# Reordering the steps of a software pipeline for multi-group cross-attention on one core

## The chip, the cores and the metric

The kernel runs on one core of a Trainium2 chip. The metric is the device time of one execution in microseconds (us). The engines are named as the profile names them: PE is the matrix engine (PEld its weight loads), ACT the scalar engine, DVE the vector engine, POOL the GpSimd engine, and SP issues DMAs. Each engine runs its own instruction list in order; they wait for one another through semaphores.

## What is computed

`x` is (16, 512, 640) and the context is (16, 512, 1024). Twenty heads of 32 channels attend to four groups of context tokens, each with its own key and value weights and its own softmax:

```python
q = _heads(hidden_states @ to_q_w)
h_txt = _sdpa(q, _heads(ehs_txt @ to_k_w), _heads(ehs_txt @ to_v_w))               # 77 tokens
h_obj = _sdpa(q, _heads(ehs_obj @ to_k_object_w), _heads(ehs_obj @ to_v_object_w)) # 4
h_oth = _sdpa(q, _heads(ehs_oth @ to_k_others_w), _heads(ehs_oth @ to_v_others_w)) # 4
h_ip = _sdpa(q, _heads(ehs_ip @ to_k_ip_w), _heads(ehs_ip @ to_v_ip_w))            # 427
out = _merge(h_txt) + _merge(h_obj) + _merge(h_oth) + _merge(h_ip)
out = out @ to_out_w + to_out_b + hidden_states
```

All of it is float32. Products with weights, and the scores, are made precise by splitting each operand into a high and a low part and adding three partial products.

## The kernel before, in words

There are two programs one behind the other. `project_context` makes all keys and values and takes the first 934 us of the span; the change does not touch it. `attend` does the rest. It works on 80 units; a unit is one batch with one block of 128 channels, which is four heads.

A unit passes through these operations:

- `queries`: 15 matmuls of 512 columns into the one PSUM tile `m_ps` (L845). `keep_queries` on DVE (L1032, L1035) scales them and splits them into `q_out`; its second instruction raises the semaphore `q_lo`. SP then copies them into `qpack` (L681).
- `scores`: 8 pairs of matmuls into the double buffer `s_ps` (L796), with the query tokens on the partitions. For each pair `pair_max` on DVE takes the row maximum (L984) and copies the 85 columns of the three small groups to `small` (L991); `ip_sums` on ACT takes the exponentials of the 427 columns of the last group and sums them (two L926 activations, each with a read of the accumulator).
- the small groups, in two halves: `small_max` on DVE (L998, L999), `less_max` on POOL (L766, L767), `small_exp` on ACT (L934), `small_sums` on DVE (L1005, L1006).
- `logs_of` on ACT (L943), `neg_lse` and `turn_lse` on DVE (L1012 to L1025), and `pack_lse` on SP, which puts the negated logarithm of the sums into extra rows of `qpack` (L688).
- `scores_t`: the scores again, now transposed and less the logarithm, 8 pairs of matmuls ("duos") into the single buffer `st_ps` (L810); `prob` on ACT takes their exponentials (L918).
- `values`: 4 times 4 matmuls with probabilities against values into `o_ps` (L824, two passes each in the trace); `heads_hi` and `heads_lo` on DVE split the result (L1045, L1050).
- `output`: 15 matmuls of 512 columns into the same `m_ps` (L868), nine slots after the unit's queries; `add_output` on DVE (L1057) adds bias and residual and raises `y_added`.

The order is written out by hand. Each engine runs `slot(m)` for m from 0 to 88, and each slot has eight steps, k from 0 to 7. A slot holds the work of one unit at each stage of the pipeline: queries of unit m, scores of units m-2 and m-1, transposed scores of m-4 and m-3, values of m-4, output of m-9. On PE a step is one duo of `scores_t`, at even steps one block of `values`, then one pair of `scores`, with pieces of `queries` and `output` at the places that the tables `Q_AHEAD`, `Q_BEHIND`, `Y_AHEAD` and `Y_BEHIND` name (ahead of that pair, or behind it). Each table maps a step to a range of the 15 products. On ACT a step is `prob` and `ip_sums`; on DVE it is `pair_max`.

Since queries and outputs share `m_ps`, they alternate. The first product of an output waits until DVE has taken the queries out (`q_lo`), and the first product of the next queries waits until DVE has taken the output out (`y_added`). A pair of `scores` waits for the exponentials of the pair two before it (`s_exp`), and a duo of `scores_t` waits for the exponentials of the duo before it (`p_done`).

## Time and profile before

| | |
|---|---|
| median of 3 runs | 2585.89 us (2582.41 to 2586.15) |
| the profiled execution | 2585.89 us, span 2584.0 us |
| busy over the span | PE 97%, PEld 71%, ACT 66%, DVE 62%, POOL 16% |
| busy from 1162 us on, by 40 slices of the span | PE, ACT and DVE at 9 tenths nearly throughout |

The span is the time from the first to the last instruction; the remaining 1.9 us lie around it. The figures over the span mix the two programs: ACT and DVE are little used in the first and heavily in the second. A row of the timeline is: start in us, duration in us, engine, line, operation, what it writes and reads, the number of instructions merged into the row and, in brackets, how long the engine had been idle and what released it. Consecutive instructions of an engine overlap in the records (a matmul's record includes its way through the array), so the pace of an engine is the distance between starts, not the sum of durations.

### The profile page before, as it was taken

To read this page: it belongs to the slowest core of one execution; us is meant where nothing else is said; L and a number is where in the kernel's file an instruction comes from. 1 tells how busy PE (TensorE), PEld (TensorE's weight loads), DVE (VectorE), ACT (ScalarE), POOL (GpSimd) and SP (SyncE) were. 2 spreads that over 40 slices of the span, in tenths; PEclk is the share of its full clock that TensorE was granted. 3 is DMA by queue.
4 is the path that set the end of the run, shared out by engine and by line. 5 is a ranking of instruction groups with operands and counts; after the bars stand their busy time and mean duration, and the time that the engine had idled before them with its cause. 6 is when DMAs were issued, how large, how long until landed. Compare 5 with 4: busy or idle time off the path is not lost.

```text
span 2584.0 us, 37371 instructions
## 1 busy us (share of the span) xinstructions
PE 2495.0 (97%) x13125; PEld 1844.4 (71%) x13125; DVE 1605.4 (62%) x2964; ACT 1707.9 (66%) x3830; POOL 408.5 (16%) x564
## 2 busy tenths in 40 slices
PE   8999999999999956999999999999999999999997
PEld 7999999999999944456666666666666666666654
DVE  3131111112121127889999999999999999999991
ACT  3131212212121116999999999999999999999992
POOL 0000000000000021321321321321321231232210
PEclk9999999999999987899999999999999999999999
DMA  9473333233232235666666666766776676666741
GB/s 235 127 243 125 119 115 122 102 119 114 95 130 96 102 106 114 120 131 126 147 147 126 149 149 123 157 143 124 153 146 124 149 147 134 143 142 139 141 101 59
DMA packets 287618, 341.25 MB, mean 132 GB/s; under 512 B 89406, under 2 KB 181694, under 8 KB 287430
## 3 DMA queue, kind: packets, MB, share of 16 engines
q1 hardware_dynamic: 234032, 275.93, 47.8%
q10 hardware_dynamic: 53398, 62.93, 7.4%
q8 instruction: 104, 1.70, 0.3%
q14 instruction: 84, 0.69, 0.1%
HBM read 186.71 MB, written 83.89 MB: 105 GB/s over the span
## 4 chain that ended last, share of the span: by engine, by line
PE 57%; ACT 3%; DVE 1%; DMA 1%; issue 1%; SPq 0%; DVEq 0%
PE s_ps L796 13%; PE st_ps L810 12%; PE o_ps L824 12%; PE m_ps L845 11%; PE m_ps L868 10%; ACT s_ps L926 2%; ACT probs L918 1%; DVE kpack L970 0%; DVE negmax L984 0%; DMA qpack<-q_out 0%; DMA small<-in_group_rows 0%; ACT small L934 0%; DMA out<-in_xT 0%; DVE out L1057 0%; DVE wo L975 0%
## 5 line engine op out<-in xcount | busy, mean ns | idle before, releaser
L926 ACT ACTIVATE s_ps<-s_ps,negmax 128x427 f32<-128x427 f32 x1280 | 762.0, 601 | 43.9 <-DVE small L991 43.9
L984 DVE TENSOR_REDUCE negmax<-s_ps 128x2 f32<-128x854 f32 x640 | 667.0, 1042 | 85.2 <-PE s_ps L796 85.0
L918 ACT ACTIVATE probs<-st_ps 128x1024 f32<-128x1024 f32 x640 | 662.4, 1035 | 57.7 <-PE st_ps L810 51.6
L796 PE MATMUL s_ps<-kpack,qpack 96*128 96x512 f32 x1280 | 438.9, 425 | 25.5 <-ACT s_ps L926 19.4
L464 PE MATMUL v_ps<-w_split,ctx_split 128*128 128x320 f32 (+2 forms) x3072 | 453.7, 309 | 1.5 <-DVE w_split L386 1.5
L464 PEld LDWEIGHTS v_ps<-w_split,ctx_split 128*128 128x128 f32 (+2 forms) x3072 | 451.4, 186 | 2.5 <-DVE w_split L386 1.8
L447 PE MATMUL k_ps<-ctx_split,w_split 128*128 128x428 f32 (+2 forms) x2280 | 428.0, 349 | 5.1 <-DVE ctx_split L386 4.6
L810 PE MATMUL st_ps<-qpack,kpack 104*128 104x512 f32 x1280 | 418.1, 408 | 13.6 <-ACT probs L918 12.7
L447 PEld LDWEIGHTS k_ps<-ctx_split,w_split 128*128 128x128 f32 x2280 | 409.6, 189 | 21.0 <-DVE ctx_split L386 4.9
L796 PEld LDWEIGHTS s_ps<-kpack,qpack 96*128 96x128 f32 x1280 | 215.8, 192 | 281.8 <-ACT s_ps L926 236.9
L391 DVE TENSOR_TENSOR k_out<-k_ps,k_out 128x427 fp32r<-128x427 f32 (+2 forms) x97 | 56.0, 578 | 532.9 <-ACT k_out L287 532.9
L766 POOL TENSOR_TENSOR small<-small,negmax 128x616 f32<-128x616 f32 x160 | 196.1, 1226 | 1162.5 <-DVE negmax L999 1162.5
L845 PE MATMUL m_ps<-xs,wq 128*128 128x512 f32 x1200 | 349.9, 401 | 26.3 <-DVE wq L975 24.8
L824 PE MATMUL o_ps<-probs,vt 128*32 128x512 f32 x2560 | 346.0, 613 | 1.1 <-ACT probs L918 1.1
L810 PEld LDWEIGHTS st_ps<-qpack,kpack 104*128 104x128 f32 x1280 | 228.8, 191 | 151.1 <-ACT probs L918 103.2
L868 PE MATMUL m_ps<-heads,wo 128*128 128x512 f32 x1200 | 317.4, 396 | 5.3 <-DVE out L1057 3.7
L308 ACT ACTIVATE v_out<-v_ps 128x640 f32<-128x640 f32 (+1 forms) x64 | 45.2, 706 | 386.6 <-PE v_ps L464 386.6
L845 PEld LDWEIGHTS m_ps<-xs,wq 128*128 128x128 f32 x1200 | 231.4, 193 | 82.2 <-issue 25.0
L926 ACT ACTIVATION_READ_ACCUMULATOR s_ps<-s_ps,negmax 128x1 f32 x1280 | 281.0, 220 | 0.0
L868 PEld LDWEIGHTS m_ps<-heads,wo 128*128 128x128 f32 x1200 | 224.7, 190 | 63.3 <-issue 5.7
L287 ACT ACTIVATE k_out<-k_ps 128x427 fp32r<-128x427 f32 (+2 forms) x97 | 49.2, 507 | 280.0 <-PE k_ps L447 262.3
L991 DVE COPY small<-s_ps 128x170 f32<-128x170 f32 x640 | 207.3, 324 | 0.0
(54 smaller groups left out, 1437.7 us busy)
## 6 DMA issues: line engine op xcount, KB each, us to landing
kpack<-kT SPq DMA_DIRECT2D x240, 256.0 KB, 5.0
qpack<-q_out SPq DMA_DIRECT2D x240, 256.0 KB, 5.7
kT<-k_out ACTq DMA_DIRECT2D x160, 217.5 KB, 2.2
ctx_split_raw<-in_ctxT SPq DMA_DIRECT2D x128, 214.0 KB, 4.5
xs_raw<-in_xT SPq DMA_DIRECT2D x80, 256.0 KB, 4.9
out<-in_xT SPq DMA_DIRECT2D x80, 256.0 KB, 5.7
out_yT<-out SPq DMA_DIRECT2D x80, 256.0 KB, 3.4
v_ip_rows<-v_out ACTq DMA_DIRECT2D x48, 320.0 KB
```

The costliest lines, as they stand in the source:

```text
L447: last = nc.tensor.matmul(k_place(run, m)[:, 0:n], w[W[name][0]][:, pw, q, m * P:(m + 1) * P], c[run % 2][:, px, q, a:a + n], start=(q == ...
L464: last = nc.tensor.matmul(v_ps[0:rows, v0 % 2, half, 0:CH // 2], c[run % 2][:, px, q, a:a + rows], w[W[name][0]][:, pw, q, half * (CH // 2 ...
L766: nc.gpsimd.tensor_tensor(txt, txt, over_keys(m_txt, N_TXT), ALU.add).then_inc(sm_sub, 1)
L796: last = nc.tensor.matmul(s_ps[:, n % 2, z, :], qpack[0:ROWS_S, r, j, t * P:(t + 1) * P], kpack[0:ROWS_S, r, j, :], start=True, stop=True)
L810: last = nc.tensor.matmul(st_ps[:, z, :], kpack[0:ROWS_ST, r, j, kt * P:(kt + 1) * P], qpack[0:ROWS_ST, r, j, :], start=True, stop=True)
L824: last = nc.tensor.matmul(o_ps[j * HD:(j + 1) * HD, :], vt[:, r, kt, j * HD:(j + 1) * HD], probs[:, (ITEMS * u + HPU * kt + j) % PR, :], s ...
L845: last = nc.tensor.matmul(m_ps[:, :], wq[:, pw, c, cols], xs[:, px, c, :], start=(n == 0), stop=(n == PRODUCTS - 1))
L868: last = nc.tensor.matmul(m_ps[:, :], wo[:, pw, z, cols], heads[:, (w // QC * QC + z) % HR, po, :], start=(n == 0), stop=(n == PRODUCTS - 1))
L918: nc.scalar.activation(probs[:, at:at + 2, :], st_ps[:, :, :], ACT.Exp).then_inc(p_done, 1)
L926: last = nc.scalar.activation(s_ps[:, n % 2, z, SMALL:TOK], s_ps[:, n % 2, z, SMALL:TOK], ACT.Exp, bias=negmax[:, r, IP, j, t:t + 1], accu ...
L984: nc.vector.tensor_reduce(negmax[:, r, IP, j, t0:t0 + 2], s_ps[:, n % 2, :, SMALL:TOK], AX_X, ALU.max, negate=True).then_inc(s_max, 1)
L991: nc.vector.tensor_copy(small[:, w:w + 2, :], s_ps[:, n % 2, :, 0:SMALL]).then_inc(s_max, 1)
```

## The change

Nothing is computed differently. The order of the steps of a slot changes on all five engines:

- PE: pieces of `queries` and `output` are all placed ahead of the pair of scores, in runs of 7, 2 and 6 (queries, steps 5, 6, 7) and 6, 2 and 7 (output, steps 1, 2, 3). The fourth block of `values` (step 6) goes ahead of the pair as well.
- DVE: `heads_hi` moves from the start of step 0 of the next slot to the start of step 7, and `heads_lo` behind step 7's `pair_max`; `small_max` and `small_sums` of the first half and `add_output` each move one step later, `small_max` of the second half too.
- ACT: `small_exp` runs behind steps 4 and 7 and not behind steps 3 and 0; `logs_of` at step 2 and not 1.
- POOL: `less_max` at steps 4 and 7, behind `split_x`; the last chunk of `x` is split at step 5.
- SP: three chunks of the next batch of `x` are loaded behind `pack_keys`, and the last two at the start of the next slot, ahead of `pack_queries`.

```diff
-Q_AHEAD = {5: (4, 8), 7: (11, 13)}
-Q_BEHIND = {4: (0, 4), 5: (8, 11), 7: (13, 15)}
-X_STEPS = {0: (0,), 1: (1,), 2: (2,), 3: (3,), 4: (4,)}
+Q_STEPS = {5: (0, 7), 6: (7, 9), 7: (9, 15)}
+X_STEPS = {0: (0,), 1: (1,), 2: (2,), 3: (3,), 5: (4,)}
-Y_AHEAD = {1: (0, 5), 3: (10, 15)}
-Y_BEHIND = {1: (5, 10)}
+Y_STEPS = {1: (0, 6), 2: (6, 8), 3: (8, 15)}
@@ sync, slot
+                if m > 0 and m % QC == 0 and unit(m):
+                    load_x(m, range(X_EARLY, QC))
                 if unit(m - 1):
                     pack_queries(m - 1)
...
-                if (m + 1) % QC == 0 and unit(m + 1):
-                    load_x(m + 1, range(X_EARLY))
                 if m > 0 and unit(m):
                     pack_keys(m)
                 if (m + 1) % QC == 0 and unit(m + 1):
-                    load_x(m + 1, range(X_EARLY, QC))
+                    load_x(m + 1, range(X_EARLY))
@@ gpsimd, slot
-                    if k in (3, 6) and unit(m - 2):
-                        less_max(m - 2, k // 6)
                     if m % QC == 0 and unit(m):
                         for c in X_STEPS.get(k, ()):
                             split_x(m, c)
+                    if k in (4, 7) and unit(m - 2):
+                        less_max(m - 2, k // 7)
@@ tensor
+            def products_at(m, k):
+                if k in Q_STEPS and unit(m):
+                    queries(m, range(*Q_STEPS[k]))
+                if k in Y_STEPS and unit(m - Y_LAG):
+                    output(m - Y_LAG, range(*Y_STEPS[k]))
...
-                    if k in (0, 2, 4) and unit(m - 4):
+                    if k % 2 == 0 and unit(m - 4):
                         values(m - 4, k // 2)
-                    products_at(m, k, Q_AHEAD, Y_AHEAD)
+                    products_at(m, k)
                     u, p = pair_at(m, k + 1) if k + 1 < STEPS else pair_at(m + 1, 0)
                     if unit(u):
                         scores(u, p)
-                    products_at(m, k, Q_BEHIND, Y_BEHIND)
-                    if k == 6 and unit(m - 4):
-                        values(m - 4, k // 2)
@@ scalar, slot
-                    if k == 1 and unit(m - 3):
+                    if k == 2 and unit(m - 3):
                         logs_of(m - 3)
...
-                    if k == 0 and unit(m - 3):
-                        small_exp(m - 3, 1)
-                    if k == 3 and unit(m - 2):
-                        small_exp(m - 2, 0)
+                    if k in (4, 7) and unit(m - 2):
+                        small_exp(m - 2, k // 7)
@@ vector, slot
-                    if k == 0 and unit(m - 5):
-                        heads_hi(m - 5)
-                        heads_lo(m - 5)
+                    if k == 7 and unit(m - 4):
+                        heads_hi(m - 4)
...
-                    if k in (2, 5) and unit(m - 2):
-                        small_max(m - 2, k // 5)
-                    if k == 3 and unit(m - Y_LAG):
+                    if k in (3, 6) and unit(m - 2):
+                        small_max(m - 2, k // 6)
+                    if k == 4 and unit(m - Y_LAG):
                         add_output(m - Y_LAG)
-                    if k == 4 and unit(m - 2):
+                    if k == 5 and unit(m - 2):
                         small_sums(m - 2, 0)
+                    if k == 7 and unit(m - 4):
+                        heads_lo(m - 4)
```

The first place is PE around the boundary of two slots, from the pair of scores that step 7 issues (it is the pair of the next slot's step 0) to the first product of the output. Before:

```order
L796 MATMUL s_ps<-kpack,qpack 128x512 [waits s_exp]
L796 MATMUL s_ps<-kpack,qpack 128x512
L845 MATMUL m_ps<-xs,wq 128x512 x2
L810 MATMUL st_ps<-qpack,kpack 128x512 [waits p_done]
L810 MATMUL st_ps<-qpack,kpack 128x512
L824 MATMUL o_ps<-probs,vt 32x512 [waits p_done,o_lo,v_in2]
L824 MATMUL o_ps<-probs,vt 32x512 x3
L796 MATMUL s_ps<-kpack,qpack 128x512 [waits s_exp]
L796 MATMUL s_ps<-kpack,qpack 128x512
L810 MATMUL st_ps<-qpack,kpack 128x512 [waits p_done]
L810 MATMUL st_ps<-qpack,kpack 128x512
L868 MATMUL m_ps<-heads,wo 128x512 [waits q_lo,o_lo]
```

And after:

```order
L843 MATMUL m_ps<-xs,wq 128x512 x6
L794 MATMUL s_ps<-kpack,qpack 128x512 [waits s_exp]
L794 MATMUL s_ps<-kpack,qpack 128x512
L808 MATMUL st_ps<-qpack,kpack 128x512 [waits p_done]
L808 MATMUL st_ps<-qpack,kpack 128x512
L822 MATMUL o_ps<-probs,vt 32x512 [waits p_done,o_lo,v_in1]
L822 MATMUL o_ps<-probs,vt 32x512 x3
L794 MATMUL s_ps<-kpack,qpack 128x512 [waits s_exp]
L794 MATMUL s_ps<-kpack,qpack 128x512
L808 MATMUL st_ps<-qpack,kpack 128x512 [waits p_done]
L808 MATMUL st_ps<-qpack,kpack 128x512
L866 MATMUL m_ps<-heads,wo 128x512 [waits q_lo,o_lo]
```

The last two products of the queries stood between the pair of scores and the output; now all of them stand ahead of the pair.

The second place is DVE over the same boundary, from the pair of step 7 to the queries. L984 and L991 (after: L977 and L984) are one `pair_max`. Before:

```order
L984 TENSOR_REDUCE negmax<-s_ps 128x2 [waits s_done]
L991 COPY small<-s_ps 128x170
L1045 CAST heads<-o_ps 128x512 [waits y_done,pv_done]
L1050 TENSOR_TENSOR heads<-o_ps,heads 128x512 [waits o_hi]
L984 TENSOR_REDUCE negmax<-s_ps 128x2 [waits s_done]
L991 COPY small<-s_ps 128x170
L1032 TENSOR_SCALAR q_out<-m_ps 128x512 [waits q_packed1,q_acc]
L1035 SCALAR_TENSOR_TENSOR q_out<-m_ps,q_out 128x512 [waits q_hi]
```

And after:

```order
L1038 CAST heads<-o_ps 128x512 [waits y_done,pv_done]
L977 TENSOR_REDUCE negmax<-s_ps 128x2 [waits s_done]
L984 COPY small<-s_ps 128x170
L1043 TENSOR_TENSOR heads<-o_ps,heads 128x512 [waits o_hi]
L977 TENSOR_REDUCE negmax<-s_ps 128x2 [waits s_done]
L984 COPY small<-s_ps 128x170
L1025 TENSOR_SCALAR q_out<-m_ps 128x512 [waits q_packed1,q_acc]
L1028 SCALAR_TENSOR_TENSOR q_out<-m_ps,q_out 128x512 [waits q_hi]
```

The two parts of the heads have moved apart, around step 7's pair; step 0's pair is still the last thing ahead of the queries.

The third place is ACT from the second half's exponential (L929 after) to the logarithm. Before, the exponential stands one step ahead of the logarithm and behind step 0's pair; after, it stands behind step 7's pair:

```order
L929 ACTIVATE small<-small 128x680 [waits sm_sub]
L913 ACTIVATE probs<-st_ps 128x1024 [waits pv_done,st_done]
L921 ACTIVATE s_ps,sums<-s_ps,negmax 128x427 [waits s_max]
L921 ACTIVATE s_ps,sums<-s_ps,negmax 128x427
L913 ACTIVATE probs<-st_ps 128x1024 [waits pv_done,st_done]
L921 ACTIVATE s_ps,sums<-s_ps,negmax 128x427 [waits s_max]
L921 ACTIVATE s_ps,sums<-s_ps,negmax 128x427
L913 ACTIVATE probs<-st_ps 128x1024 [waits pv_done,st_done]
L938 ACTIVATE logs<-sums 128x64 [waits lse_step,s_exp,sm_sum]
```

The exponential now stands directly ahead of step 0's `prob`, and two more `prob` lie between it and the logarithm.

## Rows read from the trace of the kernel before

**Rows 1.** Windows: engines' busy us, then granted clock, DMA share and GB/s.
```profile
1143.00:1162.00 19.00, 19.00 (x98) 11.75 (x94) 17.47 (x34) 18.49 (x44) 8.54 (x11) 1.00 0.80 177
```

**Rows 2.** Timeline, DVE, the first half of keep_queries in four slots.
```profile
1019.84 0.68 DVE L1032 TENSOR_SCALAR q_out<-m_ps 128x512 fp32r<-128x512 f32 x1
...
1123.63 0.68 DVE L1032 TENSOR_SCALAR q_out<-m_ps 128x512 fp32r<-128x512 f32 x1
...
1162.00 0.68 DVE L1032 TENSOR_SCALAR q_out<-m_ps 128x512 fp32r<-128x512 f32 x1
...
2486.83 0.68 DVE L1032 TENSOR_SCALAR q_out<-m_ps 128x512 fp32r<-128x512 f32 x1
```

**Rows 3.** Timeline, PE, from step 7 to step 1 of the next slot.
```profile
1525.03 0.62 PE L796 MATMUL s_ps<-kpack,qpack 96*128 96x512 f32 x2
...
1525.96 0.63 PE L810 MATMUL st_ps<-qpack,kpack 104*128 104x512 f32 x2
1526.53 1.07 PE L824 MATMUL o_ps<-probs,vt 128*32 128x512 f32 x8
1527.52 0.73 PE L796 MATMUL s_ps<-kpack,qpack 96*128 96x512 f32 x2
1528.10 0.63 PE L810 MATMUL st_ps<-qpack,kpack 104*128 104x512 f32 x2
1528.56 1.33 PE L868 MATMUL m_ps<-heads,wo 128*128 128x512 f32 x5
1529.73 0.40 PE L796 MATMUL s_ps<-kpack,qpack 96*128 96x512 f32 x1
```

**Rows 4.** Timeline, PEld, the weight loads of the first output products.
```profile
1528.42 1.04 PEld L868 LDWEIGHTS m_ps<-heads,wo 128*128 128x128 f32 x5
```

**Rows 5.** Timeline, DVE, from heads_lo to the queries of that boundary.
```profile
1525.02 0.69 DVE L1050 TENSOR_TENSOR heads<-o_ps,heads 128x512 fp32r<-128x512 f32 x1
1525.69 1.05 DVE L984 TENSOR_REDUCE negmax<-s_ps 128x2 f32<-128x854 f32 x1
1526.65 0.33 DVE L991 COPY small<-s_ps 128x170 f32<-128x170 f32 x1
1526.89 0.68 DVE L1032 TENSOR_SCALAR q_out<-m_ps 128x512 fp32r<-128x512 f32 x1
1527.61 0.69 DVE L1035 SCALAR_TENSOR_TENSOR q_out<-m_ps,q_out 128x512 fp32r<-128x512 f32 x1
```

**Rows 6.** Timeline, the first unit: products that waited for keep_queries.
```profile
961.94 0.69 DVE L1035 SCALAR_TENSOR_TENSOR q_out<-m_ps,q_out 128x512 fp32r<-128x512 f32 x1
962.68 1.46 PEld L845 LDWEIGHTS m_ps<-xs,wq 128*128 128x128 f32 x7 [2.01 <-DVE q_out L1035]
```

**Rows 7.** Timeline, PE and ACT, a prob that waited for its duo.
```profile
1521.96 0.63 PE L810 MATMUL st_ps<-qpack,kpack 104*128 104x512 f32 x2
1522.63 1.02 ACT L918 ACTIVATE probs<-st_ps 128x1024 f32<-128x1024 f32 x1 [0.35 <-PE st_ps L810]
```

**Rows 8.** Timeline, ACT, steps 0 and 1 of a slot.
```profile
1507.66 1.03 ACT L918 ACTIVATE probs<-st_ps 128x1024 f32<-128x1024 f32 x1
1508.57 0.61 ACT L926 ACTIVATE s_ps<-s_ps,negmax 128x427 f32<-128x427 f32 x1
...
1509.75 0.80 ACT L934 ACTIVATE small<-small 128x680 f32<-128x680 f32 x1
1510.41 1.05 ACT L918 ACTIVATE probs<-st_ps 128x1024 f32<-128x1024 f32 x1
```

**Rows 9.** Timeline, SP's issue of pack_lse.
```profile
1513.77 2.96 SPq L688 DMA_DIRECT2D qpack<-lse_t  x4
```

**Rows 10.** DMA share in 40 slices of 1507 to 1527 us, in tenths.
```profile
DMA  0000001999998999983210200399678997898999
```

**Rows 11.** Windows of two slots without output, columns as in rows 1.
```profile
1060.00:1079.00 19.00, 17.04 (x83) 8.56 (x79) 17.05 (x33) 18.58 (x44) 2.99 (x4) 1.00 0.58 101
1079.00:1101.00 22.00, 20.46 (x79) 10.35 (x79) 16.81 (x32) 18.35 (x43) 2.99 (x4) 0.77 0.47 86
```

More of the change, by code:

```diff
@@ L871, in output @@
                     last.then_inc(y_done, 1)
-            def products_at(m, k, q_at, y_at):
-                if k in q_at and unit(m):
-                    queries(m, range(*q_at[k]))
-                if k in y_at and unit(m - Y_LAG):
-                    output(m - Y_LAG, range(*y_at[k]))
+            def products_at(m, k):
[3 more added lines that the diff above has]
+                    output(m - Y_LAG, range(*Y_STEPS[k]))
             def slot(m):
```

## The prediction, made before the changed kernel ran

> **What bounds the kernel now.** I read the windows first. In 1143 to 1162 us, a stretch of the part in which every stage of the pipeline has a unit, PE is busy 19.00 of 19.00 us at a granted clock of 1.00, ACT 18.49 and DVE 17.47 [rows 1]. That is too close to call from busy shares, so the second view is the cadence: the first half of `keep_queries` runs once per slot, at 1162.00 and, 69 slots later, at 2486.83 [rows 2], so a full slot takes 1324.83 / 69 = 19.20 us. The third is the timeline of PE, to see whether those 19.20 us are work or waits. Two matmuls of 512 columns take 0.46 to 0.47 us from start to start (1528.10 to 1528.56, and 1525.03 to 1525.96 for four), five take 1.17 (1528.56 to 1529.73), 0.234 each. A duo ahead of values takes 0.57, a block of values 0.99, and the pair behind it 0.58, 0.11 more than a pair elsewhere, because its first weight load has nothing to hide behind [rows 3]. A slot has 16 matmuls of scores, 16 of transposed scores and 30 products, so 62 x 0.234 = 14.5 us, and 4 blocks of values at (0.57 - 0.47) + 0.99 + 0.11 = 1.2, 4.8 us: 19.3, the cadence. So in a full slot PE never waits; 19.20 us is its floor. Slots without output are another matter: there PE is busy 17.04 of 19.00 us, and the clock is at 1.00 in one and at 0.77 in the next [rows 11].
>
> **What the change can't win.** It removes no instruction from PE, and puts the same number of blocks of values between 128-row matmuls, so each full slot keeps the 19.20 us floor. The evener spread over the steps is of use to ACT and DVE alone, and neither is the bound. So the sum has only costs in it, but for the slots at the start and the end.
>
> **The cost: the hand-over of `m_ps`.** The first product of the output waits for `q_lo`, which `keep_queries` raises behind step 0's `pair_max`. I measure both sides from the pair of scores that this `pair_max` reads (S0, 1525.03).
> - DVE: `pair_max` starts 0.66 behind S0 (1525.69), the queries 1.20 behind that (1526.89), their second instruction 0.72 later (1527.61) and lasts 0.69 [rows 5]. The end is at S0 + 3.27.
> - PE before: two products, duo, values, pair, duo, then the output's first product at 1528.56, S0 + 3.53 [rows 3]. Its weight load starts at 1528.42, 0.12 behind the end of the DVE instruction [rows 4, 5]. It fits with next to nothing to spare.
> - PE after: no products behind S0. The path is pair 0.47, duo 0.57, values 0.99, pair 0.58, duo 0.46: S0 + 3.07. That is 0.20 ahead of the end of `keep_queries`; DVE's side is unchanged, since `pair_max` still stands ahead of the queries and starts when S0 is done.
>
> So PE now waits in every slot that has both a `keep_queries` and an output. Release to weight load was 0.05 where products did wait for this instruction (962.63 to 962.68) [rows 6] and 0.12 in rows 4 and 5; the exposed first load costs 0.11, taken from the pair behind values [rows 3]. The stall is 3.27 + 0.05 + 0.11 - 3.07 = 0.36 to 3.27 + 0.12 + 0.11 - 3.07 = 0.43; I take the middle, 0.395. The bounds are wider: with the handover at 0.05 and no refill it is 0.25, and if the whole 0.26 from the DVE end to the product's own start (1528.30 to 1528.56) is needed and the refill comes on top, 0.57. The slots are m = 9 (the first output) to 80 (the last `keep_queries`), 72 of them: 72 x 0.395 = 28.4 us, bounds 18 to 41. Nothing gives it back: all that stands behind the waiting product on PE (scores for DVE, duos for ACT) comes later by as much.
>
> **Edits that I cost at nothing, and their cover.** Slot times below count from step 0's duo, with the stall.
> - `small_exp` ahead of step 0's `prob`, and `heads_hi` (0.7) ahead of step 7's `pair_max`. From step 7's pair (S7): `pair_max` + 0.66, some 0.1 late for `heads_hi`, 1.3 to the end of its copy [rows 5], ACT's two activations 1.18, `small_exp` 0.66 [rows 8], `prob` 1.03 and about 0.15 to the next duo: 5.1 us to step 1's duo. PE's own way from S7 to it is 0.47 + 0.47 + 6 x 0.234 + 0.47 + 0.57 + 0.99 + 0.58 = 4.95. It is about 0.15 late, and right behind it is the product that waits 0.395 anyway: hidden. Were that stall not there, it would cost 0.15, 11 us in all.
> - `small_exp` behind step 4. Duo 4 to its `prob` 0.67 [rows 7], `prob` 0.91, activations 1.18, `small_exp` 0.66 [rows 8], `prob` to duo 6 1.18: 4.60. PE's way: 0.57 + 0.99 + 0.58 + 0.46 + 7 x 0.234 + 0.47 = 4.71. Margin 0.11, the thinnest.
> - Elsewhere a duo allows the next after 0.67 + 1.18 = 1.85, and the shortest step is 2.1.
> - `add_output` one step later. From the pair of step 4 to the first product of the next queries PE's way is again 3.07; DVE's is the chain above with one instruction where `keep_queries` has two: 3.27 - 0.72 + 0.23 = 2.78. Margin 0.29.
> - The fourth block of values ahead of its pair moves 1.2 us of work by one place. It waits for step 5's `prob`, which ends some 0.7 ahead of it by the walk above.
> - The logarithm one step later: `pack_lse` is issued at 1513.77 before, 7.0 us into its slot, over 2.96 us [rows 9], and the duo that needs it is at 1521.96 [rows 7], 15.2 into it. After, `prob` of step 2 starts at about 4.9 + 0.67 and ends 1.05 later, so the issue starts at about 8.1 and ends at 11.1; the duo comes at 14.7. Before, the DMA engines are idle from 1517.5 us, within 1.3 of the end of the issue at 1516.73 [rows 9, 10]; so the rows land by 12.4, with 2.3 us to spare.
> - `load_x` past `pack_keys`, its last two chunks ahead of `pack_queries` every fifth slot: `pack_queries` waits for `q_lo` until 2.8 us into the slot, and issuing two loads and the residual takes less. The chunks are multiplied at step 5 or later, over 12 us into the slot. POOL is busy 8.54 of 19 us in such a stretch [rows 1]: its moved steps are hidden.
>
> The Trainium skill ("DMA: Bandwidth & Descriptors", Queues, rings and completion order) says that on each DMA engine descriptors are consumed in ring order. By it the logarithms' packets, in every fifth slot, stand behind two more chunks of `x`. Rows 10 agree in kind: the share stays at 8 or 9 tenths until the queries are through and only then falls. By the rule the landing moves later in 16 slots; it changes no term of the sum.
>
> **Slots without output, and the tail.** The five slots from 1019.84 to 1123.63 take 103.8 us [rows 2], some near 19 us and some near 22 at the lower clock [rows 11]. ACT's 18.58 [rows 11] is their new floor at best, up to half a microsecond a slot under 19. If all keep the full clock, 5 x 19 = 95 is 9 less; if all lose it, 5 x 22 = 110 is 6 more. I take -1, with both ends in the range. After slot 80 no queries are left, so the wait on `q_lo` is gone; tail 0, give or take 2.
>
> **The sum.** Profiled execution 2585.9 (span 2584.0, the rest around it; the median of the runs is the same 2585.89) + 28.4 - 1 = 2613.3; predicted 2613 us.
>
> **The rivals.**
> - A second stall besides: the margin of 0.11 at step 6 is made of sums of rows to 0.01 and of ACT's pace, which is not constant. If it fails by 0.1 to 0.3 a slot, 7 to 22 us come on top, as they are at another place of PE's order: 2620 to 2635. For it: three engines within 1 us of each other. Against it: the margin holds with the rows as they are.
> - The clock. The stall makes PE idle once a slot, and rows 11 show a slot at 0.77 taking 22 us and not 19. If this came in full slots, 72 x 3 = 216 on top: about 2830. Against it: in 1060 to 1079 PE was idle 2 us of 19 and the clock stayed at 1.00; after the change it idles 0.4 of 19.6. The Trainium skill ("TensorE: Matmul & The Clock Gate", A second HAM failure mode: psum-queue depth-cycling) says that frequent micro-idles between groups of matmuls can make the clock oscillate; by it this rival would be the likely one. The rows bear it out for slots with five times the idle time, and not in each of those.
> - The logarithms late. All that is certain of their landing is that it was no later than the duo at 1521.96, 5.2 us behind the issue. If it took all of that, the duo would wait until 16.3 instead of 14.7: 1.6 x 80 = 128 us, about 2742. Rows 10 speak against it.
> - The wait is hidden: if PE ran a little behind its pace between S0 and the output, or the queries were taken out earlier, the change would only shuffle work under PE's floor: 2583 to 2588.
> - Faster: the evener steps free the slots without output. There PE idles, and the 11 products of steps 4 and 5 make ACT wait; spread over three steps they would not. With the full clock all through it is 9 us and with ACT's floor 2 more: 2575. It wins only if the stall at `m_ps` stays under 11 / 72 = 0.15 us a slot, below both my bounds.
>
> **Chances.** The forecast 0.62 (its own range 2602 to 2624), second stall 0.20, clock 0.03, logarithms 0.04, hidden 0.06, faster 0.05. What a measurement of this kernel can tell from no change is about 0.2%, 5 us. So slower 0.62 + 0.20 + 0.03 + 0.04 = 0.89, same 0.06, faster 0.05. The range runs from the forecast's end, less some for the start's clock, to the end of the second stall: 2598 to 2638, which leaves out about 0.18.
>
> **What would show it.** The distance between two `keep_queries` in full slots should be 19.6 and not 19.20. In the waits, PE's output line should appear as waiting for DVE's second `q_out` instruction in about 72 slots, 0.2 to 0.6 us each, as before it did not. The granted clock should stay 1.00 from 1162 us on. Waits of duos for `prob` should not grow beyond step 1's. If the cadence is 19.20, the reading of the hand-over is wrong; if it is above 19.7, there is a second stall, and the duo of step 6 is the first place to look.

## The result and the profile after

The changed kernel takes 2628.45 us (median of 4 runs, 2625.99 to 2630.26), the kernel before 2586.02 in the same session (4 runs, 2582.41 to 2596.81): a ratio of 1.0156, 95% interval 1.0126 to 1.0187. It is slower by 42.4 us. Forecast were 27 more, 2613: the direction held, and so did the whole range, 2598 to 2638. The range of the forecast proper, 2602 to 2624, did not: 15 us of the cost were not in the sum.

The profiled execution of after took 2634.56 us (span 2632.5), 6 more than the median; the accounts below are of this one execution against the one before, and so add up to a little more than 42.4.

Busy times over the span, to be held against the small table of before: the work is the same, only the span has grown from 2584.0 to 2632.5 us.

```profile
PE 2526.2 (96%) x13125; PEld 1843.3 (70%) x13125; DVE 1621.9 (62%) x2964; ACT 1716.9 (65%) x3830; POOL 408.0 (15%) x564
```

A window over one full slot, columns as in [rows 1]:

```profile
1199.80:1219.40 19.60, 19.56 (x98) 11.76 (x94) 17.57 (x35) 18.82 (x44) 3.00 (x4) 1.00 0.64 126
```

The granted clock is 1.00, so the time is not lost to the clock. PE counts as 19.56 busy of 19.60 although it waits in this slot, as shown below: a matmul's record covers its way through the array, and short waits vanish in it. The starts tell more. `keep_queries` [rows 2], now L1025, in the timeline of DVE: slot 10, four around one batch boundary, and slot 80.

```profile
1139.54 0.68 DVE L1025 TENSOR_SCALAR q_out<-m_ps 128x512 fp32r<-128x512 f32 x1
...
1417.61 0.68 DVE L1025 TENSOR_SCALAR q_out<-m_ps 128x512 fp32r<-128x512 f32 x1
...
1437.21 0.68 DVE L1025 TENSOR_SCALAR q_out<-m_ps 128x512 fp32r<-128x512 f32 x1
...
1458.88 0.68 DVE L1025 TENSOR_SCALAR q_out<-m_ps 128x512 fp32r<-128x512 f32 x1
...
1478.49 0.68 DVE L1025 TENSOR_SCALAR q_out<-m_ps 128x512 fp32r<-128x512 f32 x1
...
2530.98 0.68 DVE L1025 TENSOR_SCALAR q_out<-m_ps 128x512 fp32r<-128x512 f32 x1
```

The distances are 19.60, 21.67 and 19.61. Four full slots of five take 19.60, as forecast; the first slot of each batch takes 20.6 to 21.7. From slot 10 to slot 80 it is 1391.44 us, which is 70 x 19.60 + 19.4, so each of the 14 batch starts costs 1.39 on top. Before, slot 10's stood at 1142.80:

```profile
1142.80 0.68 DVE L1032 TENSOR_SCALAR q_out<-m_ps 128x512 fp32r<-128x512 f32 x1
```

and slot 80's at 2486.83 [rows 2]: 1344.03. The accounts: loop +47.4 (28.0 of it 70 x 0.40, and 19.4 for the batch starts), slot 10 reached 3.3 earlier, the tail behind slot 80's `keep_queries` 4.4 longer (101.5 against 97.1): 48.5, the difference of the spans.

**The ordinary slot.** PE over the boundary, to be held against [rows 3]:

```profile
1515.82 0.63 PE L794 MATMUL s_ps<-kpack,qpack 96*128 96x512 f32 x2
1516.28 0.63 PE L808 MATMUL st_ps<-qpack,kpack 104*128 104x512 f32 x2
1516.85 1.06 PE L822 MATMUL o_ps<-probs,vt 128*32 128x512 f32 x8
1517.84 0.73 PE L794 MATMUL s_ps<-kpack,qpack 96*128 96x512 f32 x2
1518.47 0.73 PE L808 MATMUL st_ps<-qpack,kpack 104*128 104x512 f32 x2
1519.24 1.62 PE L866 MATMUL m_ps<-heads,wo 128*128 128x512 f32 x6
1520.71 0.62 PE L794 MATMUL s_ps<-kpack,qpack 96*128 96x512 f32 x2
```

The end of the queries on DVE [rows 5], and the weight load released by it [rows 4]:

```profile
1517.69 0.68 DVE L1025 TENSOR_SCALAR q_out<-m_ps 128x512 fp32r<-128x512 f32 x1
1518.41 0.69 DVE L1028 SCALAR_TENSOR_TENSOR q_out<-m_ps,q_out 128x512 fp32r<-128x512 f32 x1
```
```profile
1519.21 1.23 PEld L866 LDWEIGHTS m_ps<-heads,wo 128*128 128x128 f32 x6 [0.45 <-issue]
```

From S0 at 1515.82, DVE is through at S0 + 3.28 and the load starts 0.11 later. The duo ahead of the product starts at 1518.47 and the product at 1519.24, 0.77 later, where [rows 3] have 0.46: 0.31 of the 0.40. The duo of step 1 starts 0.63 behind its pair and not 0.58, because `prob` is a little late: 0.05. Its weight load waited for that:

```profile
1518.46 0.30 PEld L808 LDWEIGHTS st_ps<-qpack,kpack 104*128 104x128 f32 x2 [0.33 <-ACT probs L913]
```

The rest is refill: the six products take 1.47 from start to start and not 6 x 0.234 = 1.40. The three add up to 0.43; the remainder of the slot runs 0.03 quicker than before, which leaves the 0.40. The profile puts the 0.45 down to "issue", not to `q_out`, so the waits view doesn't name the semaphore; the order of starts does.

**The batch start.** DVE at step 2 of such a slot, on which nothing was to change:

```profile
1440.89 1.05 DVE L977 TENSOR_REDUCE negmax<-s_ps 128x2 f32<-128x854 f32 x1 [0.25 <-PE s_ps L794]
...
1442.56 1.27 DVE L1005 TENSOR_TENSOR neglse<-negmax,logs 128x64 f32<-128x64 f32 x1 [0.38 <-ACT logs L938]
1443.86 0.52 DVE L1008 CAST neglse<-neglse 128x64 fp32r<-128x64 f32 x1
1444.42 1.40 DVE L1010 TENSOR_TENSOR neglse<-neglse 128x64 fp32r<-128x64 f32 x1
1445.85 0.31 DVE L1018 STREAM_TRANSPOSE lse_t<-neglse 128x128 f32<-128x128 f32 x1
1446.08 1.01 DVE L977 TENSOR_REDUCE negmax<-s_ps 128x2 f32<-128x854 f32 x1
```

The three small instructions of `neg_lse` take 3.3 us from 1442.56 to 1445.82. The same ones before, in a batch start:

```profile
1531.82 0.21 DVE L1012 TENSOR_TENSOR neglse<-negmax,logs 128x64 f32<-128x64 f32 x1
1532.07 0.22 DVE L1015 CAST neglse<-neglse 128x64 fp32r<-128x64 f32 x1
1532.33 0.28 DVE L1017 TENSOR_TENSOR neglse<-neglse 128x64 fp32r<-128x64 f32 x1
```

0.8 us. And POOL, in the batch start after:

```profile
1440.54 1.28 POOL L755 TENSOR_TENSOR xs<-xs_raw,xs 128x512 fp32r<-128x512 f32 x1
1441.78 0.60 POOL L753 CAST xs<-xs_raw 128x512 fp32r<-128x512 f32 x1
1442.46 1.29 POOL L755 TENSOR_TENSOR xs<-xs_raw,xs 128x512 fp32r<-128x512 f32 x1
1443.69 0.61 POOL L753 CAST xs<-xs_raw 128x512 fp32r<-128x512 f32 x1
1444.38 1.29 POOL L755 TENSOR_TENSOR xs<-xs_raw,xs 128x512 fp32r<-128x512 f32 x1
```

POOL's subtractions end at 1443.75 and 1445.67, DVE's two at 1443.83 and 1445.82: each of DVE's ends about 0.1 after POOL's, whatever its own work. Before, POOL was idle then: it waited in `less_max` for `row_max`, which DVE makes behind `neg_lse`, and the splits stood behind that.

```profile
1528.33 1.30 POOL L757 TENSOR_TENSOR xs<-xs_raw,xs 128x512 fp32r<-128x512 f32 x1
1533.83 1.23 POOL L766 TENSOR_TENSOR small<-small,negmax 128x616 f32<-128x616 f32 x1 [4.21 <-DVE negmax L999]
...
1535.28 0.61 POOL L755 CAST xs<-xs_raw 128x512 fp32r<-128x512 f32 x1
```

From there the delay goes on by data. ACT waits 2.40 for `pair_max`, and PE for ACT:

```profile
1447.37 0.59 ACT L921 ACTIVATE s_ps<-s_ps,negmax 128x427 f32<-128x427 f32 x1 [2.40 <-DVE small L984]
```
```profile
1448.72 0.73 PE L794 MATMUL s_ps<-kpack,qpack 96*128 96x512 f32 x2 [1.28 <-ACT s_ps L921]
```

Two theories to be tested, then. H: the hand-over of `m_ps` costs 0.4 in every full slot. P: at batch starts POOL's `split_x` holds up DVE's `neg_lse`, since the edits (split 3 ahead of `less_max`, chunks loaded later) brought them together. A third edit, the logarithm a step later, moves `neg_lse` only a little: it starts 5.34 us behind `keep_queries` after and 4.92 before, and this edit was not tested by itself. The texts of what was expected, written before each run, call H theory A and P theory C. Their rival B puts the 0.40 down to the moved `small_exp` and `heads_hi`, and their rival D puts the long batch starts down to the order of SP's loads alone.

### The profile page after: what moved, and what is told of

It reads as the page before. It is cut to its first block, busy times and chain, and to the rows that moved or that the text cites. A ratio compares the mean times of both kernels' runs of the same rounds, so it can differ in the third digit from the quotient of the medians.

```text
span 2632.5 us, 37371 instructions
## 1 busy us (share of the span) xinstructions
PE 2526.2 (96%) x13125; PEld 1843.3 (70%) x13125; DVE 1621.9 (62%) x2964; ACT 1716.9 (65%) x3830; POOL 408.0 (15%) x564
## 4 chain that ended last, share of the span: by engine, by line
PE 54%; ACT 4%; DVE 4%; issue 2%; DMA 1%; SPq 0%; DVEq 0%
PE st_ps L808 11%; PE m_ps L843 11%; PE s_ps L794 11%; PE m_ps L866 11%; PE o_ps L822 10%; ACT probs L913 2%; ACT s_ps L921 2%; DVE negmax L977 1%; DVE neglse L1010 1%; DVE neglse L1005 0%; DVE neglse L1008 0%; DVE small L984 0%; DMA small<-in_group_rows 0%; DMA qpack<-q_out 0%; DVE kpack L963 0%
## 5 line engine op out<-in xcount | busy, mean ns | idle before, releaser
L977 DVE TENSOR_REDUCE negmax<-s_ps 128x2 f32<-128x854 f32 x640 | 665.3, 1039 | 126.7 <-PE s_ps L794 124.9
L794 PE MATMUL s_ps<-kpack,qpack 96*128 96x512 f32 x1280 | 426.2, 415 | 39.1 <-ACT s_ps L921 32.8
L794 PEld LDWEIGHTS s_ps<-kpack,qpack 96*128 96x128 f32 x1280 | 230.1, 191 | 227.1 <-issue 115.6
L843 PE MATMUL m_ps<-xs,wq 128*128 128x512 f32 x1200 | 331.6, 407 | 27.8 <-DVE wq L968 26.2
L866 PE MATMUL m_ps<-heads,wo 128*128 128x512 f32 x1200 | 332.1, 409 | 9.4 <-DVE out L1050 4.9
L843 PEld LDWEIGHTS m_ps<-xs,wq 128*128 128x128 f32 x1200 | 224.4, 193 | 140.1 <-issue 90.2
L866 PEld LDWEIGHTS m_ps<-heads,wo 128*128 128x128 f32 x1200 | 216.9, 191 | 143.7 <-issue 101.7
L984 DVE COPY small<-s_ps 128x170 f32<-128x170 f32 x640 | 207.5, 324 | 0.0
```

What stands on the lines that cost most here:

```text
L794: last = nc.tensor.matmul(s_ps[:, n % 2, z, :], qpack[0:ROWS_S, r, j, t * P:(t + 1) * P], kpack[0:ROWS_S, r, j, :], start=True, stop=True)
L843: last = nc.tensor.matmul(m_ps[:, :], wq[:, pw, c, cols], xs[:, px, c, :], start=(n == 0), stop=(n == PRODUCTS - 1))
L866: last = nc.tensor.matmul(m_ps[:, :], wo[:, pw, z, cols], heads[:, (w // QC * QC + z) % HR, po, :], start=(n == 0), stop=(n == PRODUCTS - 1))
L977: nc.vector.tensor_reduce(negmax[:, r, IP, j, t0:t0 + 2], s_ps[:, n % 2, :, SMALL:TOK], AX_X, ALU.max, negate=True).then_inc(s_max, 1)
L984: nc.vector.tensor_copy(small[:, w:w + 2, :], s_ps[:, n % 2, :, 0:SMALL]).then_inc(s_max, 1)
```

## The experiments

Each was timed on one chip with the kernel before, whose median was 2582.75 beside the first four experiments of the table, 2584.75 beside the next four and 2582.8 beside the last two. Kernels of different sessions are therefore compared by ratio or by the loop, which is the time from slot 10's `keep_queries` to slot 80's in the one profiled execution of each. All times are in us.

| | median (lowest to highest), runs | ratio to before, 95% | ordinary slot | loop |
|---|---|---|---|---|
| before | 2586.02 (2582.41 to 2596.81), 4 | | 19.20 | 1344.03 |
| after | 2628.45 (2625.99 to 2630.26), 4 | 1.0156 (1.0126 to 1.0187) | 19.60 | 1391.44 |
| a_two_behind | 2612.43 (2608.65 to 2616.77), 5 | 1.0108 (1.0091 to 1.0126) | 19.34 | 1377.04 |
| b_two_ahead | 2615.71 (2613.01 to 2618.62), 5 | 1.0122 (1.0105 to 1.0139) | 19.63 | 1373.92 |
| a_split_late | 2609.23 (2603.3 to 2613.61), 6 | 1.0095 (1.0076 to 1.0114) | 19.61 | 1376.32 |
| a_both | 2592.93 (2588.8 to 2597.4), 10 | 1.0035 (1.0023 to 1.0046) | 19.34 | 1358.08 |
| b_split_early | 2589.87 (2581.81 to 2592.82), 12 | 1.0015 (1.0002 to 1.0028) | 19.20 | 1349.25 |
| a_exp_back | 2596.25 (2594.83 to 2600.24), 6 | 1.0048 (1.0032 to 1.0064) | 19.34 | 1363.67 |
| a_loads_too | 2587.86 (2584.34 to 2591.09), 12 | 1.0008 (0.9997 to 1.002) | 19.34 | 1354.49 |
| a_queries_first | 2624.63 (2618.91 to 2626.03), 4 | 1.0151 (1.0131 to 1.0171) | 19.47 | 1388.66 |
| b_pool_meets | 2613.27 (2608.68 to 2615.28), 4 | 1.0107 (1.0083 to 1.0131) | 19.31 | 1371.24 |
| a_seven | 2578.35 (2575.46 to 2585.74), 12 | 0.998 (0.9968 to 0.9993) | 19.24 | 1347.19 |

**After, with two products of the queries back behind the pair (a_two_behind).**

```diff
-Q_STEPS = {5: (0, 7), 6: (7, 9), 7: (9, 15)}
+Q_STEPS = {5: (0, 7), 6: (7, 9), 7: (9, 13)}
+Q_BEHIND = {7: (13, 15)}
@@ tensor, slot, behind the pair of scores
+                    if k in Q_BEHIND and unit(m):
+                        queries(m, range(*Q_BEHIND[k]))
```

> The kernel after, with the last two query products of step 7 behind the pair of scores, as before. Theory A (the output's first product waits for keep_queries, because nothing stands behind the pair any more): PE's way from that pair to the product is 3.53 us again, the 0.40 us wait of each full slot shrinks to what the chain over small_exp to step 1's duo leaves, 0 to 0.15; cadence 19.20 to 19.35 instead of 19.60, the whole 18 to 29 us faster than the kernel after: 2600 to 2611. Rival B (the 0.40 comes from small_exp and heads_hi being moved to the boundary of two slots): cadence stays 19.60, time 2628. The extra 1.0 to 2.1 us of every fifth slot stays under both.

The ordinary slot fell from 19.60 to 19.34, the batch starts stayed long (about 1.7 each, 0.3 more than in after, which puts the time 1 us above the expected range). H holds for 0.26 of the 0.40; the rest is a second, smaller thing in the ordinary slot.

**Before, with the same two products ahead of the pair (b_two_ahead).** The one edit alone, in the kernel that has none of the others.

```diff
-Q_AHEAD = {5: (4, 8), 7: (11, 13)}
-Q_BEHIND = {4: (0, 4), 5: (8, 11), 7: (13, 15)}
+Q_AHEAD = {5: (4, 8), 7: (11, 15)}
+Q_BEHIND = {4: (0, 4), 5: (8, 11)}
```

> The kernel before, with one edit: the last two query products of step 7 ahead of the pair of scores. Theory A: the wait at the output's first product appears here alone, cadence 19.60 (19.55 to 19.65), no long fifth slots, 72 x 0.40 = 29 us slower than before: 2615. Rival B (it takes the moved exponential and heads): cadence 19.20, 2586.

19.63 in every slot, 0.43 over the floor, and no long batch starts: the loop is 29.9 longer. Nothing of `small_exp` or `heads_hi` has moved here, so rival B is out. Here the profile names the wait. Waits view, then the PE timeline with its pair S0 at 1513.93:

```profile
PE m_ps L868 <- DVE q_out L1035: 13.9, 68, 0.2
```
```profile
1513.93 0.63 PE L796 MATMUL s_ps<-kpack,qpack 96*128 96x512 f32 x2
...
1517.36 1.40 PE L868 MATMUL m_ps<-heads,wo 128*128 128x512 f32 x5 [0.20 <-DVE q_out L1035]
```

68 waits of up to 0.2 are booked, 13.9 us, under half of the 29.9 lost: the product starts at S0 + 3.43, where work alone would have it at 3.07 by the sum, 0.36 earlier.

**After, with chunks 3 and 4 both split at step 5, behind `less_max` (a_split_late).**

```diff
-X_STEPS = {0: (0,), 1: (1,), 2: (2,), 3: (3,), 5: (4,)}
+X_STEPS = {0: (0,), 1: (1,), 2: (2,), 5: (3, 4)}
```

> The kernel after, with chunk 3 of x split on POOL behind less_max of step 4 and not ahead of it (only X_STEPS changes). Theory C (in the first slot of a batch, split_x on POOL runs while DVE computes neg_lse on SBUF tiles, whose instructions then take up to 1.40 us instead of 0.28, and DVE passes it on to ACT and PE): the third instruction of neg_lse is back at 0.28 in all slots; the first stays long in some, since chunk 2 is still split there. The fifth slots' extra falls from 1.39 on the mean to 0 to 0.4, the time by 14 to 19 us: 2609 to 2615. Rival D (the extra comes from the order of SP's loads, chunks landing late): no change, 2628.

The loop is 15.1 shorter than after's (ratio 1.0095 for 1.0156), at an ordinary slot that stays at 19.61; the excess over 70 such slots falls from 19.4 to 3.6. One line's durations (least, median, most, in ns) say why; L1010 in after, then here:

```profile
L1010 DVE TENSOR_TENSOR neglse<-neglse x80: 270/278/1405, 1008.0 to 2575.7; 128x64 fp32r<-128x64 f32 x80
```
```profile
L1010 DVE TENSOR_TENSOR neglse<-neglse x80: 270/278/286, 1005.7 to 2555.9; 128x64 fp32r<-128x64 f32 x80
```

The medians are alike; only the largest shows that in after 14 of the 80 took 1.39 to 1.41 us. The loads come as late here as in after, so rival D, the loads alone, is out, and P holds. The first of the three instructions still met chunk 2's split in 12 slots.

**Both edits (a_both).** The two diffs above together.

> The kernel after with both edits (two products behind the pair, chunk 3 split late). Theories A and C together: 18 to 29 and 14 to 19 us off, 2583 to 2597, cadence 19.20 to 19.35. If one of the two rivals holds, 2600 to 2611 or 2609 to 2615; if both, 2628.

The single edits shortened the loop by 14.4 and 15.1, both together by 33.4. They add up and a little more: the batch starts, 1.39 long in after, were 1.7 in a_two_behind. H and P are two costs, nearly independent.

**Before, with chunk 3 split ahead of `less_max` (b_split_early).**

```diff
-X_STEPS = {0: (0,), 1: (1,), 2: (2,), 3: (3,), 4: (4,)}
+X_STEPS = {0: (0,), 1: (1,), 2: (2, 3), 4: (4,)}
```

> The kernel before, with chunk 3 of x split on POOL ahead of less_max of step 3 (only X_STEPS changes; SP's order of loads is that of before). Theory C: split_x of that chunk now runs when it lands, about 5 us into the first slot of a batch, where DVE computes neg_lse; its instructions lengthen from 0.21 to 0.28 to as much as 1.4 us in most of 15 slots, and these slots take 0.5 to 1.3 us longer: 7 to 19 us, 2590 to 2602. Rival D (it takes the new order of loads): no change, 2583.

Less than expected: the loop is 5.2 longer. With the early loads of before, chunk 2 is split soon enough, and only chunk 3 meets `neg_lse`. In 11 slots its split lengthens the first instruction, to 1.0 us at most; in three of these the subtraction then lengthens the second, the cast, from 0.22 to 1.33. The third is never touched.

```profile
L1012 DVE TENSOR_TENSOR neglse<-negmax,logs x80: 212/217/1004, 1001.6 to 2524.7; 128x64 f32<-128x64 f32 x80
```

The order on POOL alone is a part of the cause; the full cost needs the later loads too.

**After, with both edits and the second half's `small_exp` behind step 0 (a_exp_back).** Theory E: the 0.14 left in the ordinary slot is the late `prob` of step 0, because `small_exp` stands ahead of it.

```diff
-                    if k in (4, 7) and unit(m - 2):
-                        small_exp(m - 2, k // 7)
+                    if k == 0 and unit(m - 3):
+                        small_exp(m - 3, 1)
+                    if k == 4 and unit(m - 2):
+                        small_exp(m - 2, 0)
```

> a_both with small_exp of the second half back behind step 0 of the next slot. The cadence of 19.34 in a_both and a_two_behind is 0.14 over PE's 19.20. Theory E (that is the chain pair_max, exponentials, small_exp, prob to step 1's duo, worked out at 5.1 us against 4.95): without small_exp in it the chain is 0.66 shorter and the cadence 19.20; 72 x 0.14 = 10 us less than a_both: 2583. Rival F (the hand-over of m_ps still costs 0.14): cadence stays 19.34, 2593.

E fails: still 19.34. The wait went from the duo of step 1 to that of step 2, behind ACT's longer step 0. The rival F of the expectation, that the hand-over still costs this 0.14, is no better: the first product of the output starts 0.47 behind its duo, as it does without a wait. The PE timeline at step 2, with the weight load of the duo:

```profile
1507.94 0.62 PE L795 MATMUL s_ps<-kpack,qpack 96*128 96x512 f32 x2
1508.45 0.30 PEld L809 LDWEIGHTS st_ps<-qpack,kpack 104*128 104x128 f32 x2 [0.33 <-ACT probs L916]
1508.46 0.73 PE L809 MATMUL st_ps<-qpack,kpack 104*128 104x512 f32 x2
1509.12 1.06 PE L823 MATMUL o_ps<-probs,vt 128*32 128x512 f32 x8
```

The duo is 0.52 behind its pair and not 0.47, and the values 0.66 behind the duo and not 0.57: a wait of 0.05 costs 0.14. The likely reason is that weight loads have nothing left to hide behind: the load of this duo starts 0.01 ahead of it, where that of the duo before (1505.84 to 1506.08) starts 0.24 ahead. `small_exp` takes 0.66 of ACT wherever it stands, and the idea is that the step in which it stands needs one product more on PE; the uneven tables of before gave it that. The time is 3 us above that of a_both, by the ratios: `neg_lse` now comes 0.2 later and meets chunk 2 more often, and the batch starts cost 9.9 and not 4.3.

**The same, with the loads of `x` in the order of before (a_loads_too).**

```diff
-                if m > 0 and m % QC == 0 and unit(m):
-                    load_x(m, range(X_EARLY, QC))
...
+                if (m + 1) % QC == 0 and unit(m + 1):
+                    load_x(m + 1, range(X_EARLY))
                 if m > 0 and unit(m):
                     pack_keys(m)
                 if (m + 1) % QC == 0 and unit(m + 1):
-                    load_x(m + 1, range(X_EARLY))
+                    load_x(m + 1, range(X_EARLY, QC))
```

> a_exp_back with SP's loads of x in the order of before. In a_both some first slots of a batch are still 0.4 to 0.7 longer. Theory C (chunk 2 lands late and its split meets neg_lse): with the loads earlier, chunks 0 to 2 are split before neg_lse, the extra goes, 4 to 5 us less than a_exp_back: 2578. Under rival D alone (loads, not the meeting of POOL and DVE) a_split_late could not have gained its 19 us; here it would give no more than C.

The loop is 9.2 shorter, and it is 70 x 19.34 to within 0.7: the batch starts cost nothing any more. (In the two runs without it the excess was 4.3 and 9.9.) So the load order was the other part of P. Taken together: late loads with the early split cost 19.4 (after), the early split alone 5.2 (b_split_early), the late loads alone 3.6 to 9.9, neither of them 0.7.

**After, with `keep_queries` ahead of step 0's `pair_max` (a_queries_first).** It lets go of `m_ps` earlier and keeps the rest.

```diff
+                    if k == 0 and unit(m - 1):
+                        keep_queries(m - 1)
                     u, p = pair_at(m, k)
                     if unit(u):
                         pair_max(u, p)
-                    if k == 0 and unit(m - 1):
-                        keep_queries(m - 1)
```

> The kernel after, with keep_queries ahead of step 0's pair_max on DVE. Theory A: q_lo comes 1.2 us earlier, the output's first product waits no more; but that pair_max starts about 1 us late, its exponentials and step 1's prob with it, and the duo of step 2 waits about 0.4 instead. Cadence 19.4 to 19.7, time 2615 to 2635: the wait changes place. If DVE's lateness is absorbed, cadence 19.34 and 2610.

The ordinary slot is 19.47, 0.13 less than after and 0.27 over the floor. The hand-over is free, which gave back 0.26 in a_two_behind, but `pair_max` and what ACT makes from it come later: of the 0.27, 0.14 are the late duo of step 1, and 0.13 are new, at the duo of step 2. So half of the wait has changed its place.

**Before, with a POOL subtraction that nobody waits for (b_pool_meets).** It is extra work on a spare tile, released by the logarithm as `neg_lse` is.

```diff
+        spare = sb("spare", [P, TOK], F32)
...
+                    if k == 2 and unit(m - 3):
+                        pool.wait_ge(ln_done, m - 2)
+                        nc.gpsimd.tensor_tensor(spare[:, :], wq[:, HI, 0, 0:TOK].bitcast(F32),
+                                                wq[:, LO, 0, 0:TOK].bitcast(F32), ALU.subtract)
```

> The kernel before, with one more instruction on POOL per slot: as soon as the logarithm is done, where DVE runs neg_lse, POOL subtracts two 512-column float32 pieces of wq in SBUF into a spare tile that nothing reads (the same shape as split_x's second half, 1.3 us). Nothing waits for it. Theory C (DVE's and POOL's instructions on SBUF with two inputs exclude each other): one or two of neg_lse's instructions take about 1.0 to 1.4 us in every slot, the cadence rises from 19.20 by 0.3 to 1.2, 75 x that: 2605 to 2675. Rival D (no such exclusion, the long instructions in the kernel after had another cause, such as its DMAs): neg_lse stays at 0.21 to 0.28, time 2584.

30.5 us slower, though nothing waits for the result of the added instruction. An ordinary slot takes 19.31, 0.11 more and less than the 0.3 expected: only the first instruction is longer there, and most of it is absorbed. A batch start takes 20.7, since there the splits follow right behind; that is 19.5 of the 27.2 us by which the loop grew. Durations of the first instruction of `neg_lse` (before: median 0.21 us), then DVE and POOL in a batch start:

```profile
L1017 DVE TENSOR_TENSOR neglse<-negmax,logs x80: 224/625/637, 1003.9 to 2556.7; 128x64 f32<-128x64 f32 x80
```
```profile
1537.49 0.64 DVE L1017 TENSOR_TENSOR neglse<-negmax,logs 128x64 f32<-128x64 f32 x1
1538.17 0.52 DVE L1020 CAST neglse<-neglse 128x64 fp32r<-128x64 f32 x1
1538.72 1.39 DVE L1022 TENSOR_TENSOR neglse<-neglse 128x64 fp32r<-128x64 f32 x1
```
```profile
1536.75 1.30 POOL L774 TENSOR_TENSOR spare<-wq 128x512 f32<-128x512 f32 x1 [3.61 <-ACT logs L948]
1537.99 0.62 POOL L756 CAST xs<-xs_raw 128x512 fp32r<-128x512 f32 x1
1538.69 1.29 POOL L758 TENSOR_TENSOR xs<-xs_raw,xs 128x512 fp32r<-128x512 f32 x1
```

POOL's subtractions end at 1538.05 and 1539.98, DVE's instructions at 1538.13 and 1540.11. It is POOL's running, not its data, that delays DVE; rival D, no such meeting, is out.

**After as in a_loads_too, with seven products in ACT's long step (a_seven).** Theory G, formed from a_exp_back.

```diff
-Y_STEPS = {1: (0, 6), 2: (6, 8), 3: (8, 15)}
+Y_STEPS = {1: (0, 7), 2: (7, 8), 3: (8, 15)}
```

> a_loads_too with output products in runs of 7, 1 and 7 instead of 6, 2 and 7 in steps 1, 2 and 3. In a_exp_back and a_loads_too small_exp of the second half stands in step 0; the cadence stayed 19.34, and the wait moved from step 1's duo to step 2's: prob of step 1 ends 0.05 too late for it, and a drained PE pays 0.10 more for the first weight load. Theory G (each slot pays wherever ACT's long step meets too few products on PE): one more product in step 1, 0.23 us, covers the 0.05, cadence 19.20, 10 us less than a_loads_too: 2578, which would beat the kernel before by what the slots without output give. Rival F (a cost of the hand-over): 19.34, 2588.

The ordinary slot is 19.24, so one product more in that step gave back 0.10 of the 0.14. The 0.04 left stand at step 6, two steps behind the other `small_exp`:

```profile
1550.04 0.30 PEld L809 LDWEIGHTS st_ps<-qpack,kpack 104*128 104x128 f32 x2 [0.24 <-issue]
1550.07 0.71 PE L809 MATMUL st_ps<-qpack,kpack 104*128 104x512 f32 x2
...
1550.70 1.06 PE L823 MATMUL o_ps<-probs,vt 128*32 128x512 f32 x8
```

The values start 0.63 behind the duo and not 0.57, and the load of the duo starts only 0.03 ahead of it.

The median 2578.35 beats both kernels, the one before by 0.2% (0.1 to 0.3). The loop is still 3.2 longer than before's; in the profiled executions the gain lies ahead of slot 10 (10.2 us) and in the tail (2.3), where the granted clock differs between executions. Such a lead need not come from the edits of PE's order: b_split_early, which has the order of before there, reached slot 10 9.3 us earlier than before did. What makes the 0.2% stays open.

## Why the prediction was right, and where it fell short

The prediction was right in direction and within its whole range, and the stall that it priced is there at its price. The rest was in part luck: 2628 lies outside the forecast's own range, 2602 to 2624, and is covered only because the range was drawn on to 2638 for a second stall, whose mechanism is not the one that came.

- **PE's floor of 19.20, so no gain from the evener spread.** Right: no version went under it, the best stands at 19.24.
- **The stall at the hand-over, 0.395 a slot (0.36 to 0.43).** Right in place and size. The ordinary slot is 19.60; alone it costs 0.43 (b_two_ahead). DVE's side was read as S0 + 3.27 and is 3.28.
- **`small_exp` ahead of step 0's `prob`: 0.15 late, hidden behind the stall.** Right that it is hidden: with the stall taken away 0.14 remained (a_two_behind, 19.34). The size is luck in part: the duo is only 0.05 late (`prob` to duo took 0.05, not 0.15), and 0.09 more are lost behind it. That its old place would be free was not forecast, and isn't so under the even tables (a_exp_back).
- **"POOL is busy 8.54 of 19 us in such a stretch: its moved steps are hidden."** This is the step that failed, together with the `load_x` edit costed at nothing on the same line. It asked whether POOL had time and whether the chunks came early enough for PE, and both are so. It did not ask what POOL's work does to DVE. This term, put at nothing, is 14 x 1.39 = 19.4 us; the excess was 3.6 in a_split_late and 0.7 in a_loads_too, and a kernel with nothing but a POOL instruction more paid for the same meeting (b_pool_meets). The 15 us that the forecast was short lie here. [rows 1] could not tell; POOL's and DVE's timelines over step 2 of a batch start, laid side by side, show DVE's chain in the time in which POOL waited.
- **The rival of a second stall, 2620 to 2635, 0.20.** The number came true, the mechanism did not: it placed the stall at the duo of step 6, in every slot, and there the duo still starts 0.47 behind its pair. It came in every fifth slot, by way of DVE's `pair_max` of step 3, and PE met it first at the pair of scores that it issues in step 4. The margin of 0.11 was thin all the same: in a_seven 0.04 to 0.06 are lost at that place.
- **The clock.** The full slots stay at 1.00 with 0.4 us of waiting in 19.6. The rule of the Trainium skill named in the prediction ("TensorE: Matmul & The Clock Gate", A second HAM failure mode: psum-queue depth-cycling) isn't borne out at this dose.
- **The sign in the waits.** 72 waits of the output's line for `q_out`, of 0.2 to 0.6, were to appear. In after there is none: the profile books them as "issue". In b_two_ahead 68 appear, of at most 0.2. The distance of 19.6 was the sign that held.
- **Sums.** The 0.23 in the chain of `add_output` stands in no row; the instruction takes 0.75, which puts the end at S0 + 2.61 and not 2.78, with more to spare. 2613.3 + 128 is 2741, not 2742. In [rows 10] the DMA engines are not quite idle from 1517.5 on: the slice from 1518.0 has 2 tenths. None of this changes the forecast.
- **Logarithms late, hidden, faster.** None of them came. Of the duos, one waited for `pack_lse`, for 1.6 us, in the tail at 2581. The part ahead of slot 10 was 3.3 us shorter, where -1 was taken, and the tail 4.4 longer, where 0 give or take 2 was. In two windows without output, this one and the next, the clock was now 1.00, columns as in [rows 11]:

```profile
1063.00:1082.00 19.00, 17.43 (x83) 8.55 (x79) 16.85 (x34) 18.56 (x44) 2.99 (x4) 1.00 0.56 101
```

This was not tested by itself, and part of it differs from one execution to another: between the start of `attend`, at 934 us, and slot 10 the mean granted clock was 0.80 in before, 0.84 in after and 0.83 in b_split_early, whose PE order is that of before.

In sum: forecast +28.4 - 1; in the profiled execution +28.0 in 70 slots for the hand-over with the late duo hidden behind it, +19.4 for POOL and DVE, +1.1 for both ends.

## What to carry to other kernels

Read the engines' hand-over of a shared buffer against the same start mark on both sides; it gave 0.36 to 0.43 us for a stall from a trace in which the stall did not exist, and 0.40 and 0.43 were measured. When steps of POOL are moved, walk through what DVE does at that moment: an idle POOL is no licence, and a chain on DVE that stood in POOL's waiting time was protected by it. Where some slots differ from the others, look at the largest duration of a group and not at its mean.

## What the runs showed of the hardware

- **POOL holds up DVE on some instructions until it is through.** A DVE operation of 128x64 with two inputs in SBUF took 0.28 us by itself and up to 1.40 while POOL subtracted 128x512 (1.29), ending 0.1 after it. The cast next to it, with one input, took 0.52 for 0.22 beside POOL's cast (0.61), and 1.33 where it met the subtraction (three slots of b_split_early). POOL's own subtractions all took 1.28 to 1.30 in after. `pair_max`, which reads PSUM, keeps its duration beside such a subtraction: it took 1.05 from 1440.89, while POOL subtracted from 1440.54 to 1441.82. So does `small_sums` (L998), a reduction with one input in SBUF: 0.78 to 0.80 in 21 such meetings. The Trainium skill ("GPSIMD Engine Reference", 1. Specifications) says that the two share their access to SBUF, with contention where DVE reads two inputs from SBUF or runs in a mode that uses two ports. The rows of the two-input operations agree; whether the cast ran in such a mode no run here shows.
- **A short wait on PE costs more than its length.** 0.05 of waiting took 0.14 (a_exp_back), probably because the weight loads are then exposed. The profile books a part of this as "issue" and shows PE as busy: 68 waits of at most 0.2 stood for 29.9 us of loop time (b_two_ahead).
